# Down products of sequences 1 to 3 as three fp32r passes, with their place in the order moved

## Chip, core and metric

The kernel runs on one core of a Trainium2 chip. The metric is the device time of one execution in microseconds. The engines are TensorE (PE, with its weight loads PEld), VectorE (DVE), ScalarE (ACT), GpSimd (POOL) and SyncE (SP); each has its own queue of instructions and runs it in order, and semaphores tie them together.

## What is computed

Input is x of shape 4 x 1024 x 128: four sequences of 1024 tokens with 128 features. Four layers are added to it, each on a layer norm of x:

```python
x = x + attn_a(_layernorm(x))   # conv, pooled attention, small MLP; per sequence
x = x + ffn(_layernorm(x))      # 8 experts, summed: silu(x @ wg) * (x @ wu) @ wd, 128 -> 512 -> 128
x = x + attn_b(_layernorm(x))   # 16 heads, ALiBi
x = x + ffn(_layernorm(x))      # the same weights again
```

The end of attn_a is what the change touches:

```python
h = _ln(x, ln_boom_g, ln_boom_b)
h = gelu(h @ Wb.T + bb)         # 128 -> 512
x = x + (h @ Wu.T + bu)         # 512 -> 128: the down product
```

All is float32. The kernel runs many products as three fp32r passes: each operand is split into a high part (a cast to fp32r) and a low part (the rest), and hi·hi, hi·lo and lo·hi are summed in PSUM. Others are one plain fp32 matmul.

## The kernel before

Tokens go in 8 tiles of 512. The first ffn walks the tiles in four pairs (function `pair`, kinds first, middle, middle, last). A tile has 32 chunks of 128 hidden features (8 experts x 4), so a pair has 64 steps, 0 to 63. In step p each engine's program has a fixed piece. PE runs the gate and up products of chunk p + 2 (L1132 to L1134, six fp32r matmuls) and then the down product of chunk p (L1139 to L1141, three); it starts the latter when h_hi and h_lo of chunk p are there. ACT runs the silu of chunk p + 1 (L1609) and the cast h_hi of chunk p (L1627). DVE runs the product `hid` of chunk p + 1 (L2059) and the low part h_lo of chunk p (L2080).

Beside pair i the kernel computes attn_a of sequence i + 1, piece by piece (`sequence_step`). Sequence 0 runs ahead of the ffn, its second half partly in the first steps of pair 0 (table `LEFT`). A half u is 512 tokens. At which step a piece stands is written by hand in the table `AT` (first half, second half), to which the first pair adds `SHIFT_FIRST` = 10 and the middle pairs add 3. On every engine the piece stands behind the ffn work of the step, except on PE, where it stands ahead of it.

The pieces that matter here: `up`, four products per half into PSUM, each 128x512 (first half one per step, second half all four in one step); their bias is added by ACT or DVE on the way into `gel`, which lies in the memory `work`; `gelu`, one ACT instruction over 128x2048 of `gel` (L1533), with a table load ahead of it and another ahead of the next silu; `down` (L974), four fp32 matmuls of 128x512 summed in one bank: first half at 42, all four in one step, second half two in each of steps 44 and 45; then `y` (DVE adds bias and residual), `T13` (PE transposes), `x1` (DVE adds into x). `gelu` stands at 36 and 41. In the middle pairs that is: second Gelu in step 44, first half's down in 45, second half's in 47 and 48. In the first pair each is 7 later: 51, 52, 54, 55. `NORM_AT` says at which step the layer norm of the next tile starts (its statistics on DVE); it needs x1 of that tile, and its result is needed by PE in step 62.

The normalised input of the `up` products lies as high part in `h2T` and low part in `h2_lo`; both are free once the last `up` product has run. POOL has little to do in this stretch: two steps of each inner norm, three kinds of 128x512 operations per half (L699, L702, L706), and the reciprocal root of each tile norm. In the last pair it computes 20 of the h_lo (L807).

## Time and profile before

| | us |
|---|---|
| median of 3 runs | 1729.06 |
| lowest, highest | 1727.78, 1729.42 |
| the profiled execution's own time | 1728.12 |
| its span, first to last instruction | 1726.0 |
| PE busy | 1643.9 (95%) |
| DVE busy | 1247.0 (72%) |
| ACT busy | 1042.8 (60%) |
| POOL busy | 254.2 (15%) |

The three pairs with a sequence beside them reach from about 66 to 577 us of the span.

How to read the rows further down. A row of the timeline is: start in us, duration in us, engine, line, operation, what it writes <- what it reads, shapes, xN if N instructions are merged, and in brackets the idle time of the engine ahead of it and who ended it. Durations of matmuls are modelled and overlap, so a pace is read from the distance between starts. A row of the table by stretch is: stretch, its length, then for PE, PEld, DVE, ACT and POOL the busy time and the number of instructions, then the clock that TensorE was granted (1.00 is its 2.4 GHz level, 0.50 its 1.2 GHz level), the DMA share and GB/s. A row by line is: line, engine, operation, names, shapes, count | busy us, mean ns of one | idle time before it and who ended it.

### The profile page before, as it was taken

To read this page: it belongs to the slowest core of one execution; us is meant where nothing else is said; L and a number is where in the kernel's file an instruction comes from. 1 tells how busy PE (TensorE), PEld (TensorE's weight loads), DVE (VectorE), ACT (ScalarE), POOL (GpSimd) and SP (SyncE) were. 2 spreads that over 40 slices of the span, in tenths; PEclk is the share of its full clock that TensorE was granted. 3 is DMA by queue.
4 is the path that set the end of the run, shared out by engine and by line. 5 is a ranking of instruction groups with operands and counts; after the bars stand their busy time and mean duration, and the time that the engine had idled before them with its cause. 6 is when DMAs were issued, how large, how long until landed. Compare 5 with 4: busy or idle time off the path is not lost.

```text
span 1726.0 us, 28181 instructions
## 1 busy us (share of the span) xinstructions
PE 1643.9 (95%) x10321; PEld 1128.6 (65%) x10321; DVE 1247.0 (72%) x2150; ACT 1042.8 (60%) x1692; POOL 254.2 (15%) x471
## 2 busy tenths in 40 slices
PE   5899999999999999989999999989999999999998
PEld 3567777777777876643333333336888888888886
DVE  6678577766866777778888888874666666666665
ACT  6445755565565555567777777776555555555554
POOL 6522001200210013422212112111000000000000
PEclk8999999999999999989999999999999999999999
DMA  7000001002000023223112111100000000000000
GB/s 220 1 0 1 1 20 42 0 1 51 15 1 1 23 88 109 87 79 94 41 48 62 28 51 54 36 4 1 1 7 7 1 7 7 1 7 1 7 7 6
DMA packets 63427, 52.44 MB, mean 30 GB/s; under 512 B 7984, under 2 KB 58559, under 8 KB 63295
## 3 DMA queue, kind: packets, MB, share of 16 engines
q1 hardware_dynamic: 63120, 50.57, 10.1%
q8 instruction: 87, 1.43, 0.3%
q14 instruction: 46, 0.37, 0.1%
q10 hardware_dynamic: 174, 0.07, 0.0%
HBM read 32.40 MB, written 18.22 MB: 29 GB/s over the span
## 4 chain that ended last, share of the span: by engine, by line
PE 80%; DVE 12%; ACT 4%; issue 2%; POOL 1%; DVEq 0%; ACTq 0%; POOLq 0%
PE ps L1283 7%; PE ps L1281 7%; PE ps L1282 7%; PE ps L1244 6%; PE ps L1132 6%; PE ps L1134 6%; PE ps L1133 5%; DVE negm L2049 4%; PE ps L1109 4%; PE ps L1084 4%; PE ps L851 4%; PE ps L1307 3%; PE ps L1305 3%; PE ps L1306 3%; PE ps L1139 3%; PE ps L1141 3%
## 5 line engine op out<-in xcount | busy, mean ns | idle before, releaser
L2190 DVE SCALAR_TENSOR_TENSOR hid<-sg,ps 128x512 f32<-128x512 f32 x256 | 176.0, 687 | 186.3 <-PE ps L1283 185.2
L1694 ACT ACTIVATE sg<-ps 128x512 f32<-128x512 f32 x256 | 153.4, 599 | 239.3 <-PE ps L1283 237.6
L2059 DVE TENSOR_TENSOR hid<-sg,ps 128x512 f32<-128x512 f32 x256 | 174.9, 683 | 167.8 <-PE ps L1134 123.6
L1609 ACT ACTIVATE sg<-ps 128x512 f32<-128x512 f32 x256 | 153.5, 600 | 226.5 <-PE ps L1134 223.7
L2049 DVE TENSOR_REDUCE negp<-ps 128x2 f32<-128x1024 f32 (+2 forms) x224 | 249.4, 1147 | 43.3 <-PE ps L1072 21.5
L1603 ACT ACTIVATE pr<-ps 128x1024 f32<-128x1024 f32 (+2 forms) x208 | 197.1, 958 | 73.2 <-PE ps L1072 37.5
L1132 PE MATMUL ps<-xn_hi,w_hi 128*128 128x512 f32 x512 | 214.5, 419 | 2.0 <-DVE xn_lo L1825 2.0
L1281 PE MATMUL ps<-xn_hi,w_hi 128*128 128x512 f32 x512 | 203.2, 397 | 0.0
L1134 PE MATMUL ps<-xn_hi,w_lo 128*128 128x512 f32 x512 | 201.9, 394 | 0.0
L1283 PE MATMUL ps<-xn_hi,w_lo 128*128 128x512 f32 x512 | 201.7, 394 | 0.0
L1133 PE MATMUL ps<-xn_lo,w_hi 128*128 128x512 f32 x512 | 201.6, 394 | 0.0
L1282 PE MATMUL ps<-xn_lo,w_hi 128*128 128x512 f32 x512 | 200.7, 392 | 0.0
L2080 DVE TENSOR_TENSOR h_lo<-hid,h_hi 128x512 fp32r<-128x512 f32 x236 | 177.3, 751 | 0.0
L2195 DVE TENSOR_TENSOR h_lo<-hid,h_hi 128x512 fp32r<-128x512 f32 x256 | 175.2, 684 | 0.1
L1627 ACT CAST h_hi<-hid 128x512 fp32r<-128x512 f32 x256 | 157.2, 614 | 0.4 <-DVE hid L2059 0.4
L1700 ACT CAST h_hi<-hid 128x512 fp32r<-128x512 f32 x256 | 156.9, 613 | 0.4 <-DVE hid L2190 0.4
L1109 PE MATMUL ps<-qs,ks 63*128 63x512 bf16 (+2 forms) x720 | 113.2, 331 | 20.6 <-DVE negm L2049 12.5
L1109 PEld LDWEIGHTS ps<-qs,ks 63*128 63x128 bf16 x720 | 37.2, 93 | 144.6 <-issue 79.2
L1084 PE MATMUL ps<-ks,qs 60*128 60x512 bf16 (+2 forms) x720 | 114.4, 330 | 10.3 <-ACT pr L1603 6.5
L1603 ACT ACTIVATE pr_third<-ps 128x1024 f32<-128x1024 f32 (+2 forms) x112 | 100.9, 901 | 28.3 <-PE ps L1072 22.2
L1132 PEld LDWEIGHTS ps<-xn_hi,w_hi 128*128 128x128 f32 x512 | 96.6, 189 | 29.9 <-issue 9.8
L736 POOL TENSOR_TENSOR lnw<-mv,eps 128x4 f32<-128x4 f32 x16 | 4.1, 257 | 747.2 <-DVE mv L1806 747.2
(252 smaller groups left out, 3029.6 us busy)
## 6 DMA issues: line engine op xcount, KB each, us to landing
qs<-qd SPq DMA_DIRECT2D x60, 96.0 KB
ks<-kd SPq DMA_DIRECT2D x60, 96.0 KB
kd<-qkp SPq DMA_DIRECT2D x14, 256.0 KB, 2.9
qd<-qkp SPq DMA_DIRECT2D x7, 384.0 KB, 2.5
w_raw<-in_Wg SPq DMA_DIRECT2D x4, 512.0 KB, 7.5
w_raw<-in_Wu SPq DMA_DIRECT2D x4, 512.0 KB, 7.6
w_raw<-in_Wd SPq DMA_DIRECT2D x4, 512.0 KB, 8.6
work<-hd SPq DMA_DIRECT2D x8, 256.0 KB, 5.0
```

The lines of the kernel that those rows point to most:

```text
L1084: mm = pe.matmul(dst[e], q_of(n)[r, hp, i * P:(i + 1) * P], k_of(n)[r, hp, kc * NT:kc * NT + w], start=True, stop=not diag)
L1109: mm = pe.matmul(dst[e], k_of(n)[r, hp, j * P:(j + 1) * P], q_of(n)[r, hp, from_q:from_q + w], start=True, stop=st not in MASKED)
L1132: pe.matmul(dst, w_hi[m][:, w], xn_hi[:, h, :], start=True, stop=False)
L1133: pe.matmul(dst, w_hi[m][:, w], xn_lo[:, h, :], start=False, stop=False)
L1134: pe.matmul(dst, w_lo[m][:, w], xn_hi[:, h, :], start=False, stop=True).then_inc(f[sig], 1)
L1281: pe.matmul(dst, w_hi[m][:, w], xn_hi[:, h, :], start=True, stop=False)
L1282: pe.matmul(dst, w_hi[m][:, w], xn_lo[:, h, :], start=False, stop=False)
L1283: pe.matmul(dst, w_lo[m][:, w], xn_hi[:, h, :], start=False, stop=True).then_inc(f[sig], 1)
L1603: a.activation(pr_of(n, st)[:].rearrange("p (e a) q -> p e a q", e=2)[:, :, hps[0]:hps[-1] + 1, 0:WIDTH[st]], heads(buf, hps, WIDTH[st]), ...
L2049: v.tensor_reduce(to[:, :, hps[0]:hps[-1] + 1, i % SUB], heads(buf, hps, JOB_WIDTH[k]), AX.X, ALU.max, negate=True).then_inc(T["reduced"], 1)
L2080: v.tensor_tensor(h_lo[:, c % 2, :], hid[:, c % 4, :], h_hi[:, c % 2, :].bitcast(F32), ALU.subtract).then_inc(f["hlo"], 1)
L2190: v.scalar_tensor_tensor(hid[:, q % 4, :], sg[:, q % 2, :], 2.0, bank(up_bank(q)), ALU.mult, ALU.mult).then_inc(f["prod"], 1)
```

## The change

The down products of sequences 1 to 3 run as three fp32r passes each (new L1010 to L1012 in place of L974). For that the 512x128 weights are split once in the first pair (`w_down_hi` by ACT in step 20, `w_down_lo` by DVE in step 22, both in memory where the transposed weights lay). The Gelu's output is split for each of the 8 chunks of 512 tokens of a sequence: ACT casts the high part into the memory of the normalised input (`hidden_hi`: chunks 0 and 1 of a half in `h2T`, 2 and 3 in `h2_lo`), and POOL writes the low part over the Gelu's output (`work_lo`). Table entries: casts and subtractions at 38, 39, 40, 42 and 45, 46, 47, 48; `down` from (42, 44) to (44, 50); `y`, `T13` and `x1` follow it; the second norm of the middle pairs from 16 to 18. `gelu` stays at (36, 41). The counts of some semaphores are shifted to fit.

```diff
       "cumq": (15, 19), "kq": (17, 21), "cumk": (18, 22), "vq": (20, 24),
       "T9": (23, 26), "stats9": (23, 26), "norm9": (29, 30), "T10": (30, 31), "h3": (30, 31),
       "low3": (30, 31),
-      "up": (32, 37), "gelu": (36, 41), "down": (42, 44), "y": (43, 45), "T13": (44, 46),
-      "x1": (44, 46)}
+      "up": (32, 37), "gelu": (36, 41), "down": (44, 50), "y": (45, 51), "T13": (46, 52),
+      "x1": (46, 52)}
 
 
 UP_AT = [AT["up"][0] + c for c in range(4)] + [AT["up"][1]] * 4
 DOWN_AT = [AT["down"][0]] * 4 + [AT["down"][1] + c // 2 for c in range(4)]
 
 SHIFT_FIRST = 10
-NORM_AT = {"first": (12, 24), "middle": (10, 16), "last": (13, None)}
+HIDDEN_AT = ((38, 39, 40, 42), (45, 46, 47, 48))
+NORM_AT = {"first": (12, 24), "middle": (10, 18), "last": (13, None)}
 LOW_LATE = 13
...
     if name == "tok":
         return TOK_AT[u][c]
     if name == "hid1":
...
         return ROOTS_FIRST[name, u]
-    return b * 16 - 6 + 4 * u + (4 if name == "norm5" else 12)
+    return b * 24 - 14 + 4 * u + (4 if name == "norm5" else 12)
+
+
+def hidden_to(b, u, c):
+
+    return b * 24 - 14 + 16 + u * 4 + c + 1
+
+
+def wide_to(b, u, c):
+
+    return 4 + (b - 1) * 8 + u * 4 + c + 1
...
 SEQ_BIAS_AT, SEQ_PAR_AT, SEQ_HI_AT, SEQ_LO_AT = 7, 8, 18, 20
+DOWN_HI_AT, DOWN_LO_AT = 20, 22
 
 
...
-            sb("other_matrices", [P, (T_IN - SEQ_MATS) * P], F32, two)
+            w_down_lo = sb("w_down_lo", [P, 4 * P], F32R, two)
+            w_down_hi = sb("w_down_hi", [P, 4 * P], F32R, two)
             rinv = sb("rinv", [P, S], F32, two)
...
 
-            work = sb("work", [P, 4, S], F32, two)
+            with ExitStack() as one:
+                work = sb("work", [P, 4, S], F32, one)
+            work_lo = sb("work_lo", [P, 4, S], F32R, two)
+            gel_lo = work_lo[:].rearrange("p i (a n) -> p (i a) n", n=NT)
             a0_tok, hc_tok, cq, pq = (work[:, i, :] for i in range(4))
...
 
+        def hidden_hi(c):
+
+            return (h2T if c < 2 else h2_lo)[:, c % 2 * NT:(c % 2 + 1) * NT]
+
...
+                    for c in range(4):
+                        if now("hidden", u, c):
+                            pool.wait_ge(s["seq_wide"], wide_to(b, u, c))
+                            n = u * 4 + c
+                            g.tensor_tensor(gel_lo[:, n, :], gel[:, n, :], hidden_hi(c).bitcast(F32), ALU.subtract
+                                            ).then_inc(s["a_pool"], 1)
...
                             elif c == 0:
-                                pe.wait_ge(s["a_gel"], b * 2 + u)
+                                if first:
+                                    pe.wait_ge(s["a_gel"], 1)
                                 pe.wait_ge(s["a_hid1"], b * 4 + 4)
-                            mm = pe.matmul(bank(4) if ahead else dst, W(T_DOWN + c),
-                                           gel_first[:, c, :] if ahead else gel[:, u * 4 + c, :],
-                                           start=(c == 0), stop=(c == 3))
+                            if first:
+                                mm = pe.matmul(bank(4) if ahead else dst, W(T_DOWN + c),
+                                               gel_first[:, c, :] if ahead else gel[:, u * 4 + c, :],
+                                               start=(c == 0), stop=(c == 3))
+                            else:
+                                w = slice(c * P, (c + 1) * P)
+                                pe.wait_ge(s["a_pool"], hidden_to(b, u, c))
+                                pe.matmul(dst, w_down_hi[:, w], hidden_hi(c), start=(c == 0), stop=False)
+                                pe.matmul(dst, w_down_hi[:, w], gel_lo[:, u * 4 + c, :], start=False, stop=False)
+                                mm = pe.matmul(dst, w_down_lo[:, w], hidden_hi(c), start=False, stop=(c == 3))
                             if c == 3:
...
                                      ACT.Gelu).then_inc(s["a_gel"], 1)
+                    for c in range(4):
+                        if now("hidden", u, c):
+                            act.wait_ge(s["a_gel"], b * 2 + u)
+                            if u == 0:
+                                act.wait_ge(s["a_up"], b * 8 + 8)
+                            else:
+                                act.wait_ge(s["a_dn"], b * 2 + 1)
+                            a.copy(hidden_hi(c), gel[:, u * 4 + c, :]).then_inc(s["seq_wide"], 1)
...
                              scale=col(gain)).then_inc(s["seq_wide"], 1)
+
+            def high_part_of_down():
+
+                act.wait_ge(s["a_conv"], 4)
+                a.copy(w_down_hi[:], wt[:, T_DOWN * P:T_CONV * P]).then_inc(s["seq_wide"], 1)
...
                                 high_part_of_sequences(h * CH + c - SEQ_HI_AT)
+                            if kind == "first" and h * CH + c == DOWN_HI_AT:
+                                high_part_of_down()
...
                                     ).then_inc(s["seq_parts"], 1)
+
+            def low_part_of_down():
+
+                dve.wait_ge(s["seq_wide"], 4)
+                dve.wait_ge(s["a_dn"], 2)
+                v.tensor_tensor(w_down_lo[:], wt[:, T_DOWN * P:T_CONV * P], w_down_hi[:].bitcast(F32), ALU.subtract
+                                ).then_inc(s["seq_parts"], 1)
 
```

**PE around the second Gelu of sequence 2.** Before, from the layer's down product of step 44 to that of step 45; `work` is the Gelu's output, `wt` the weights:

```order
L1139 MATMUL ps<-h_hi,w_hi2 128x512
L1140 MATMUL ps<-h_lo,w_hi2 128x512
L1141 MATMUL ps<-h_hi,w_lo2 128x512
L974 MATMUL ps<-work,wt 128x512 x4
L1132 MATMUL ps<-xn_hi,w_hi0 128x512
L1133 MATMUL ps<-xn_lo,w_hi0 128x512
L1134 MATMUL ps<-xn_hi,w_lo0 128x512
L1132 MATMUL ps<-xn_hi,w_hi1 128x512
L1133 MATMUL ps<-xn_lo,w_hi1 128x512
L1134 MATMUL ps<-xn_hi,w_lo1 128x512
L1139 MATMUL ps<-h_hi,w_hi2 128x512
```

The same stretch with the change:

```order
L1175 MATMUL ps<-h_hi,w_hi2 128x512
L1176 MATMUL ps<-h_lo,w_hi2 128x512
L1177 MATMUL ps<-h_hi,w_lo2 128x512
L1168 MATMUL ps<-xn_hi,w_hi0 128x512
L1169 MATMUL ps<-xn_lo,w_hi0 128x512
L1170 MATMUL ps<-xn_hi,w_lo0 128x512
L1168 MATMUL ps<-xn_hi,w_hi1 128x512
L1169 MATMUL ps<-xn_lo,w_hi1 128x512
L1170 MATMUL ps<-xn_hi,w_lo1 128x512
L1175 MATMUL ps<-h_hi,w_hi2 128x512
L1176 MATMUL ps<-h_lo,w_hi2 128x512
L1177 MATMUL ps<-h_hi,w_lo2 128x512
```

The four products between the two down products of the layer are gone from here; they stand two steps further on, as twelve fp32r matmuls. In the changed kernel the layer's lines are L1168 to L1170 and L1175 to L1177.

**ACT around the second Gelu of sequence 2.** Before, steps 43 to 45:

```order
L1609 ACTIVATE sg<-ps 128x512
L1627 CAST h_hi<-hid 128x512
L1609 ACTIVATE sg<-ps 128x512
L1627 CAST h_hi<-hid 128x512
L1533 ACT_TABLE_LOAD
L1533 ACTIVATE work<-work 128x2048
L1609 ACT_TABLE_LOAD
L1609 ACTIVATE sg<-ps 128x512
L1627 CAST h_hi<-hid 128x512
```

With the change (ACT's ffn lines are L1658 and L1676, the Gelu L1569, the new casts L1578):

```order
L1658 ACTIVATE sg<-ps 128x512
L1676 CAST h_hi<-hid 128x512
L1578 CAST h2_lo<-work 128x512
L1658 ACTIVATE sg<-ps 128x512
L1676 CAST h_hi<-hid 128x512
L1569 ACT_TABLE_LOAD
L1569 ACTIVATE work<-work 128x2048
L1658 ACT_TABLE_LOAD
L1658 ACTIVATE sg<-ps 128x512
L1676 CAST h_hi<-hid 128x512
L1578 CAST h2_lo<-work 128x512
```

The third cast of the half stands ahead of the second Gelu's step, the fourth behind the silu and h_hi that follow it; the Gelu itself has kept its place.

**ACT behind the first Gelu of sequence 2.** Before, from the table load back to the h_hi of step 41:

```order
L1609 ACT_TABLE_LOAD
L1609 ACTIVATE sg<-ps 128x512
L1627 CAST h_hi<-hid 128x512
L1609 ACTIVATE sg<-ps 128x512
L1627 CAST h_hi<-hid 128x512
```

With the change:

```order
L1658 ACT_TABLE_LOAD
L1658 ACTIVATE sg<-ps 128x512
L1676 CAST h_hi<-hid 128x512
L1658 ACTIVATE sg<-ps 128x512
L1676 CAST h_hi<-hid 128x512
L1578 CAST h2T<-work 128x512
```

The first cast stands behind the h_hi of step 41; POOL's first subtraction waits for it.

## Rows read from the trace of the kernel before

**Rows 1.** The page, busy time of each engine over the span

```profile
PE 1643.9 (95%) x10321; PEld 1128.6 (65%) x10321; DVE 1247.0 (72%) x2150; ACT 1042.8 (60%) x1692; POOL 254.2 (15%) x471
```

**Rows 2.** Busy time by stretch, around the down products of sequence 2

```profile
340.00:410.00 70.00, 69.66 (x294) 53.39 (x293) 43.27 (x77) 41.44 (x66) 1.21 (x2) 1.00 0.00 1
```

**Rows 3.** Timeline, steps 44 to 46 of pair 1: second Gelu, first half's down

```profile
360.77 1.28 ACT L1533 ACT_TABLE_LOAD   x1
...
362.07 1.91 ACT L1533 ACTIVATE work<-work 128x2048 f32<-128x2048 f32 x1
362.22 0.39 PE L1139 MATMUL ps<-h_hi,w_hi 128*128 128x512 f32 x1
...
362.92 3.59 PE L974 MATMUL ps<-work,wt 128*128 128x512 f32 x8
...
364.00 1.28 ACT L1609 ACT_TABLE_LOAD   x1
...
365.29 0.60 ACT L1609 ACTIVATE sg<-ps 128x512 f32<-128x512 f32 x1
...
365.79 0.61 ACT L1627 CAST h_hi<-hid 128x512 fp32r<-128x512 f32 x1
...
366.60 0.69 DVE L2080 TENSOR_TENSOR h_lo<-hid,h_hi 128x512 fp32r<-128x512 f32 x1
...
367.74 0.61 ACT L1627 CAST h_hi<-hid 128x512 fp32r<-128x512 f32 x1
367.74 0.39 PE L1139 MATMUL ps<-h_hi,w_hi 128*128 128x512 f32 x1
...
368.55 0.68 DVE L2080 TENSOR_TENSOR h_lo<-hid,h_hi 128x512 fp32r<-128x512 f32 x1
...
369.82 0.39 PE L1139 MATMUL ps<-h_hi,w_hi 128*128 128x512 f32 x1
```

**Rows 4.** Timeline, steps 6 and 7 of pair 0: second Gelu of sequence 0

```profile
83.98 0.39 PE L1139 MATMUL ps<-h_hi,w_hi 128*128 128x512 f32 x1
...
84.68 1.62 PE L868 MATMUL ps<-par,wt 128*128 128x1 f32 x14
...
88.35 0.68 DVE L2080 TENSOR_TENSOR h_lo<-hid,h_hi 128x512 fp32r<-128x512 f32 x1
...
89.18 0.47 PE L1139 MATMUL ps<-h_hi,w_hi 128*128 128x512 f32 x1 [1.39 <-ACT h_hi L1627]
```

**Rows 5.** Timeline, steps 40 and 41 of pair 1, behind the first Gelu

```profile
353.47 0.61 ACT L1627 CAST h_hi<-hid 128x512 fp32r<-128x512 f32 x1
...
355.07 0.69 DVE L2080 TENSOR_TENSOR h_lo<-hid,h_hi 128x512 fp32r<-128x512 f32 x1
...
355.90 0.47 PE L1139 MATMUL ps<-h_hi,w_hi 128*128 128x512 f32 x1 [0.19 <-DVE h_lo L2080]
```

**Rows 6.** Timeline, pair 0: a POOL operation and a VectorE low part

```profile
155.21 1.28 POOL L699 TENSOR_TENSOR work<-work,rinv 128x512 f32<-128x512 f32 x1 [1.82 <-DVE work L1897]
...
155.63 1.41 DVE L2080 TENSOR_TENSOR h_lo<-hid,h_hi 128x512 fp32r<-128x512 f32 x1
```

**Rows 7.** Groups by line: POOL's low parts in the last pair

```profile
L807 POOL TENSOR_TENSOR h_lo<-hid,h_hi 128x512 fp32r<-128x512 f32 x20 | 25.7, 1283 | 26.3 <-ACT h_hi L1627 26.3
```

**Rows 8.** Timeline of PE at the end of the first ffn

```profile
750.63 0.66 PE L851 MATMUL ps<-ident,yS 128*128 128x128 f32 x4 [1.83 <-ACT yS L1658]
...
755.11 0.27 PE L1092 MATMUL ps<-identb,mq 128*48 128x128 bf16 x1 [2.94 <-POOL mq L774]
```

**Rows 9.** Busy time and granted clock by stretch, at three gaps

```profile
88.00:90.00 2.00, 0.82 (x4) 0.71 (x5) 2.00 (x4) 1.16 (x3) 0.00 (x0) 1.00 0.00 0
752.00:756.00 4.00, 1.06 (x11) 0.51 (x11) 2.41 (x12) 2.26 (x4) 3.62 (x9) 0.71 0.43 153
756.00:760.00 4.00, 3.15 (x24) 1.43 (x24) 3.94 (x7) 1.94 (x2) 0.33 (x1) 0.50 0.93 309
764.00:768.00 4.00, 3.92 (x30) 0.94 (x29) 2.34 (x4) 2.35 (x4) 0.00 (x0) 1.00 0.56 150
```

## What I expect of it

> **What bounds the kernel now.** I began with the page. TensorE (PE) is busy 1643.9 us of a span of 1726.0 us; no other engine comes near (DVE 72%, ACT 60%) [rows 1]. An average over stages doesn't settle the stretch that the change touches, so I asked for the busy time of the stretch in which the down products of sequence 2 lie. There PE is busy 69.66 of 70 us, ScalarE (ACT) 41 us, VectorE (DVE) 43 us and GpSimd (POOL) 1.2 us, at a granted clock of 1.00 [rows 2]. So every microsecond of PE work or of PE waiting added there moves the end, and every one taken away is a gain.
>
> The next view is the timeline around the down products. The first matmul of the layer's own down product (L1139) marks each step. An undisturbed step is 369.82 − 367.74 = 2.08 us for nine fp32r matmuls [rows 3], 0.231 us each. (The durations in the rows, 0.39 us, overlap; only distances between starts count.) The step that holds the four fp32 products of the first half is 367.74 − 362.22 = 5.52 us [rows 3].
>
> The reader should see one more thing there. Between 360.77 and 365.29 us ACT does nothing for the layer: table load 1.28, Gelu of the second half 1.91, table load back 1.28 us. Only then come the silu, the high part h_hi, DVE's product and its low part h_lo, which ends at 366.60 + 0.69 = 367.29 us [rows 3]. PE can't run its own down product of this step before that. It starts it at 367.74 us without having waited: the four fp32 products were exactly the work that lay over ACT's absence.
>
> **The change, part by part.**
>
> Price of a product. Four fp32 products cost 5.52 − 2.08 = 3.44 us, 0.86 each. Three fp32r passes of the same shape cost 3 × 0.231 = 0.693 us. Saved: 0.167 us a product, 24 products: 4.0 us. The Trainium skill (page "FP8 and Floating Point Precision") counts true FP32 as four passes through the array. That alone would make a product 4 × 0.231 = 0.92 us and the saving 5.5 us; the trace has 0.86, and I use the trace.
>
> The move of the first half. Its products go two steps later, while the second Gelu stays where it was. Between the layer's down product of the step before and that of the next, in the Gelu's shadow, PE now has only six gate and up matmuls, 6 × 0.231 = 1.39 us. The trace of before has this case: at sequence 0's second Gelu no down product lies beside it. There the distance between the two L1139 is 89.18 − 83.98 = 5.20 us, although PE filled part of it with 14 tiny bias matmuls; h_lo was late and PE sat idle 1.39 us [rows 4]. The length is ACT's and DVE's chain, not PE's: the same chain in [rows 3] ends at 367.29 us, and 0.15 us later (as from 88.35 + 0.68 to 89.18 in [rows 4]) PE could start, 367.44 − 362.22 = 5.2 us. So the step shrinks only from 5.52 to 5.20 us, with PE idle about 5.20 − 2.08 = 3.1 us in it (some 2.9 in the record, as the matmul ends overlap), and the four products are paid again in full two steps later, 4 × 0.693 = 2.77 us. First half, per sequence: −0.32 + 2.77 = +2.45 us.
>
> The move of the second half. Six steps later there is no Gelu and nothing waits for it soon: it only gets cheaper, 4 × 0.167 = −0.67 us. T13 and x1 follow by one step as before; the norm of the next tile is moved two steps and its input is needed some ten steps on.
>
> Together +1.78 us a sequence, +5.3 us for three.
>
> The 24 casts on ACT. One costs 0.61 us, and ACT starts every 0.50 us when it has work (365.29 to 365.79) [rows 3]. A step of 2.08 us has two ACT instructions of this kind; a third fits. The fourth cast of the first half comes behind silu and h_hi of the stalled step, so it delays only the next silu, by 0.5 us, for which PE's own late restart leaves room. Price: 0. Without that cover it would be up to 0.5 us a cast.
>
> The 24 subtractions on POOL. POOL's 128x512 subtraction takes 1.28 us [rows 7]. Here DVE pays. DVE's h_lo (two inputs in SBUF) takes 0.69 us alone [rows 3], but 1.41 us when it starts inside a POOL operation of this kind: POOL ran from 155.21 to 156.49, and h_lo, begun at 155.63, ended at 157.04 us, 0.55 us after POOL [rows 6]. So the price depends on when POOL starts. In an undisturbed step h_hi starts with L1139 (both 367.74), so the new cast would end 0.50 + 0.61 = 1.11 us after it; h_lo has then been running since 0.81 us (368.55) [rows 3]. POOL comes behind it, at about 1.5 us, and is done at 2.8, before the next h_lo at 2.08 + 0.81 = 2.9: no cost. At the step of the first cast it is different, since DVE is late there. ACT has h_hi at 353.47, the cast would run until about 354.6, POOL from 354.65 to 355.9. DVE's h_lo starts at 355.07, and PE already waits for it (0.19 us of idle at 355.90) [rows 5]. Blocked, it ends at 355.92 + 0.55 = 356.47 instead of 355.75 us: +0.7 us on PE, of which the next step's small wait gives back 0.1. I take +0.6 us a sequence, 1.9 us in all. Bounds: 0 (if POOL comes behind h_lo everywhere) and 0.7 + 7 × 0.3 = 2.8 us a sequence, 8.4 in all (every other h_lo blocked too; an undisturbed h_lo ends at 368.55 + 0.68 = 369.23 us, 0.6 before L1139 and so 0.4 before PE would notice, which leaves 0.3 of the 0.7).
>
> One-off work in the first pair: a cast and a subtraction of 128x512 for the weights, 0.6 and 0.7 us, in steps in which PE has no wait: 0. DVE's subtraction isn't near a long POOL operation.
>
> **Sum.** 5.3 + 1.9 = +7.2 us. The profiled execution took 1728.12 us, so by the sum 1735.3. The median of the runs shown is 0.94 us above it; on that scale 1729.06 + 7.2 = 1736.3 us.
>
> **Rivals.**
>
> *No lock cost.* If the subtractions always come behind h_lo, only the move is paid: 1729.06 + 5.3 = 1734.4 us. For: the undisturbed steps leave a gap just large enough. Against: the late h_lo of [rows 5], which I expect to be caught in all three sequences.
>
> *The Gelu stays covered, faster than before.* If PE didn't lose the 3.1 us, only the saving would be left: −4.0 us, 1725.1 us. It decides at a loss of 8 × 0.167 = 1.3 us a sequence: below that the change wins. It would need DVE's h_lo of the step to end 1.8 us earlier than in [rows 4], though the same ACT instructions stand ahead of it. I see nothing that does it.
>
> *The clock falls.* The three new gaps of some 2.9 us are the longest in the sequences' stretch. At gaps of 1.83 and 2.94 us around 752 us [rows 8] the granted clock fell: 0.71 on average over 752 to 756 us, 0.50 behind it, 1.00 again from 764, so about 10 us at half; at the single gap of 1.39 us it stayed at 1.00 [rows 9]. Where PE is the bound, 10 us at the 1.2 GHz level do 5 us of work, so one fall costs 5 us: 1736.3 + 5 = 1741.3 us; three: 1751.3 us. For: the length is that of the second gap there. Against: there two gaps came close together, and here full steps of matmuls stand on both sides. The Trainium skill (page "TensorE: Matmul & The Clock Gate", section "Why this matters for your kernels") warns that a long idle gap between bursts takes the clock back to half; by it this rival would be the likeliest.
>
> *ACT falls behind.* If each of the 24 casts reached PE with its 0.5 us: +12 us on top of 5.3, some 1746 us. ACT's 41 of 70 us, plus 8 × 0.5 a sequence, speak against it.
>
> **Chances.** Forecast 0.50; no lock cost 0.22; one or more clock falls 0.13; ACT behind 0.05; Gelu covered 0.05; partly covered, so that gain and loss about cancel, 0.05. A measurement of this kernel can tell about 0.2% (3.5 us) from no change: below 1725.6 is faster, above 1732.5 slower. Faster 0.05, same 0.05, slower 0.90. The range takes in the forecast, the case without lock cost less the scatter of the runs, one clock fall, and the upper bound of the lock cost (1729.06 + 5.3 + 8.4 = 1742.8): 1732.5 to 1743 us.
>
> **What would show it.** Right: in each of the three sequences a gap on PE of about 2.9 us ahead of the layer's own down product, in the step behind the second Gelu's, released by DVE's h_lo or ACT's h_hi; steps of 5.2, 4.85 (2.08 + 2.77) and twice 3.47 us (2.08 + 1.39); h_lo of 1.2 to 1.4 us at the first cast of each sequence with a PE wait of 0.7 to 0.9 us; clock 1.00 throughout. Wrong: no gap behind the Gelu would fell the main term; h_lo always 0.69 us the second; a clock of 0.50 within the sequences' stretch would mean 5 us more each time; PE waiting for ACT's h_hi at several casts would mean that ACT is the bound.

## The result, and the profile with the change

| | before | changed |
|---|---|---|
| median, us | 1729.42 (5 runs) | 1739.05 (5 runs) |
| lowest, highest | 1727.78, 1730.96 | 1737.99, 1741.70 |
| ratio, 95% interval | | 1.0059 [1.0046, 1.0072] |
| profiled execution, its span | 1728.12, 1726.0 | 1741.70, 1739.3 |

The change costs 9.6 us. The page of the changed kernel, busy time of each engine over the span:

```profile
PE 1645.4 (95%) x10345; PEld 1134.0 (65%) x10345; DVE 1253.5 (72%) x2151; ACT 1055.4 (61%) x1717; POOL 288.3 (17%) x495
```

Beside [rows 1], PE is busy only 1.5 us more and the span is 13.3 us longer: most of what was added is waiting. (The 1.5 us is a balance: the three passes save some 4 us of PE's work, and three stretches at the lower clock, below, add some 4.7.) The waiting shows in the busy time by stretch, 70 us around the down products of sequence 2 (columns as in [rows 2]):

```profile
345.00:415.00 70.00, 65.87 (x290) 52.51 (x289) 43.99 (x75) 43.68 (x70) 12.28 (x10) 1.00 0.00 1
```

PE is now idle 4.1 us of the 70, where before it was idle 0.3 us [rows 2]. POOL has 12.3 us to do instead of 1.2. The timeline shows where PE waits. First the step behind the second Gelu of sequence 2 (steps 45 and 46 of pair 1; L1175 is the layer's own down product, L1569 the Gelu, L1676 h_hi, L2138 h_lo, L1578 and L733 the new casts and subtractions; the casts into `h2_lo` appear as h_lo):

```profile
365.97 1.28 ACT L1569 ACT_TABLE_LOAD   x1
...
367.27 1.92 ACT L1569 ACTIVATE work<-work 128x2048 f32<-128x2048 f32 x1
367.42 0.39 PE L1175 MATMUL ps<-h_hi,w_hi 128*128 128x512 f32 x1
...
369.20 1.28 ACT L1658 ACT_TABLE_LOAD   x1
...
370.99 0.61 ACT L1676 CAST h_hi<-hid 128x512 fp32r<-128x512 f32 x1
...
371.80 0.68 DVE L2138 TENSOR_TENSOR h_lo<-hid,h_hi 128x512 fp32r<-128x512 f32 x1
...
372.19 1.44 POOL L733 TENSOR_TENSOR work_lo<-work,h_lo 128x512 fp32r<-128x512 f32 x1 [6.28 <-ACT h_lo L1578]
...
372.63 0.47 PE L1175 MATMUL ps<-h_hi,w_hi 128*128 128x512 f32 x1 [2.96 <-DVE h_lo L2138]
...
374.78 0.40 PE L1175 MATMUL ps<-h_hi,w_hi 128*128 128x512 f32 x1
...
375.47 0.39 PE L1010 MATMUL ps<-h2T,w_down_hi 128*128 128x512 f32 x1
...
379.65 0.40 PE L1175 MATMUL ps<-h_hi,w_hi 128*128 128x512 f32 x1
```

ACT's chain is that of [rows 3]: load, Gelu, load, silu, h_hi, then DVE's h_lo. It ends at 372.48 us. PE had no products to run meanwhile and stood idle for 2.96 us. The step took 372.63 − 367.42 = 5.21 us against 5.52 in [rows 3], the next one 2.15, and the one with the first half's twelve fp32r matmuls 379.65 − 374.78 = 4.87 us.

Then the first cast of the sequence (step 41), which stands against [rows 5]:

```profile
358.35 0.62 ACT L1578 CAST h2T<-work 128x512 fp32r<-128x512 f32 x1
...
359.11 1.29 POOL L733 TENSOR_TENSOR work_lo<-work,h2T 128x512 fp32r<-128x512 f32 x1 [30.21 <-ACT h2T L1578]
...
359.44 1.51 DVE L2138 TENSOR_TENSOR h_lo<-hid,h_hi 128x512 fp32r<-128x512 f32 x1
...
361.10 0.47 PE L1175 MATMUL ps<-h_hi,w_hi 128*128 128x512 f32 x1 [1.02 <-DVE h_lo L2138]
...
361.47 1.49 DVE L2138 TENSOR_TENSOR h_lo<-hid,h_hi 128x512 fp32r<-128x512 f32 x1
```

POOL had started its subtraction at 359.11. DVE's h_lo, begun at 359.44, took 1.51 instead of 0.69 us and ended 0.55 us behind POOL. PE waited 1.02 us for it, before 0.19 [rows 5]. The h_lo after it is caught too (1.49 us), but PE doesn't wait there. The Trainium skill (page "SBUF — State Buffer", section "SBUF: two separate sides") says that VectorE, with two inputs in SBUF, and GpSimd share a port pair as an exclusive lock, held for the whole instruction. The trace agrees: h_lo isn't slowed in proportion, it ends when POOL is done and a little more.

Last, TensorE's granted clock. The falls below are not in the profile of before (busy time and clock by stretch, behind the Gelu's gap of pair 0 and at two places of the attention):

```profile
217.60:221.00 3.40, 3.22 (x8) 2.57 (x9) 1.49 (x3) 0.95 (x3) 1.18 (x1) 0.50 0.00 0
1170.00:1173.20 3.20, 3.20 (x20) 0.26 (x12) 1.01 (x9) 2.19 (x3) 0.00 (x0) 0.50 0.01 4
1187.00:1190.20 3.20, 3.20 (x28) 0.72 (x24) 0.28 (x1) 1.51 (x2) 0.76 (x2) 0.50 0.00 0
```

Three times TensorE ran at its 1.2 GHz level for 3.4 us: from 217.6 us, the very end of the gap of 2.98 us of sequence 1, and from 1169.9 and 1186.9 us in the attention, which the change doesn't touch.

**The account of the profiled execution**, from the distance between the layer's down products step by step (pair 1; pair 2 agrees with it within 0.03 us a step, pair 0 is taken up below):

| step of pair 1 | before | changed | difference |
|---|---|---|---|
| 41: first cast | 2.43 | 3.26 | +0.83 |
| 45: behind the second Gelu | 5.52 | 5.21 | −0.31 |
| 46 | 2.08 | 2.15 | +0.07 |
| 47: first half's products now | 4.24 | 4.87 | +0.63 |
| 48: second half's went from here | 3.78 | 2.08 | −1.70 |
| 52: transposes went from here | 2.51 | 2.08 | −0.43 |
| 53: second half's products, two | 2.08 | 3.47 | +1.39 |
| 54: the other two, and transposes | 2.08 | 3.91 | +1.83 |
| 55: transposes of T13 | 2.08 | 2.51 | +0.43 |
| sum | | | +2.74 |

Three sequences like this: +8.2 us. Pair 0 has the same differences seven steps later and two more: the clock adds 1.55 us at 217.6 us (step 53 took 3.63 instead of 2.08 us), and step 57 is 0.25 us longer, which the run without subtractions, below, has too (0.23) and whose cause isn't shown. So the steps without the clock come to some +8.5 us. The last down product of the first ffn starts 9.9 us later (757.8 against 747.8 us). The other 3.4 us of the span's 13.3 come behind it, with two clock falls of the same length. The profiled execution is the slowest of its five; the median has some 1.1 us on top of 8.5.

### The profile page after: what moved, and what is told of

It is laid out like the page before. It is cut to its first block, busy times and chain, and to the rows that moved or that the text cites. A ratio compares the mean times of both kernels' runs of the same rounds, so it can differ in the third digit from the quotient of the medians.

```text
span 1739.3 us, 28304 instructions
## 1 busy us (share of the span) xinstructions
PE 1645.4 (95%) x10345; PEld 1134.0 (65%) x10345; DVE 1253.5 (72%) x2151; ACT 1055.4 (61%) x1717; POOL 288.3 (17%) x495
## 3 DMA queue, kind: packets, MB, share of 16 engines
q8 instruction: 87, 1.43, 0.3%
## 4 chain that ended last, share of the span: by engine, by line
PE 79%; DVE 12%; ACT 5%; issue 2%; POOL 1%; DMA 0%; DVEq 0%; SPq 0%; ACTq 0%; POOLq 0%
PE ps L1317 7%; PE ps L1318 7%; PE ps L1319 7%; PE ps L1280 6%; PE ps L1168 5%; PE ps L1170 5%; PE ps L1169 5%; PE ps L1145 4%; DVE negm L2107 4%; PE ps L1120 4%; PE ps L879 3%; PE ps L1343 3%; PE ps L1341 3%; PE ps L1342 3%; PE ps L1175 3%; PE ps L1177 3%
## 5 line engine op out<-in xcount | busy, mean ns | idle before, releaser
L1658 ACT ACTIVATE sg<-ps 128x512 f32<-128x512 f32 x256 | 153.5, 600 | 219.7 <-PE ps L1170 216.9
L1168 PE MATMUL ps<-xn_hi,w_hi 128*128 128x512 f32 x512 | 211.6, 413 | 2.0 <-DVE xn_lo L1876 2.0
L1170 PE MATMUL ps<-xn_hi,w_lo 128*128 128x512 f32 x512 | 202.3, 395 | 0.0
L2138 DVE TENSOR_TENSOR h_lo<-hid,h_hi 128x512 fp32r<-128x512 f32 x236 | 183.5, 778 | 0.0
L2255 DVE TENSOR_TENSOR h_lo<-hid,h_hi 128x512 fp32r<-128x512 f32 x256 | 175.0, 683 | 0.1
L1676 ACT CAST h_hi<-hid 128x512 fp32r<-128x512 f32 x256 | 157.2, 614 | 0.4 <-DVE hid L2117 0.4
L1175 PE MATMUL ps<-h_hi,w_hi 128*128 128x512 f32 x256 | 104.4, 408 | 19.4 <-DVE h_lo L2138 14.7
L1168 PEld LDWEIGHTS ps<-xn_hi,w_hi 128*128 128x128 f32 x512 | 96.9, 189 | 28.1 <-issue 8.3
```

The costliest lines, as they stand in the source:

```text
L1168: pe.matmul(dst, w_hi[m][:, w], xn_hi[:, h, :], start=True, stop=False)
L1170: pe.matmul(dst, w_lo[m][:, w], xn_hi[:, h, :], start=False, stop=True).then_inc(f[sig], 1)
L2138: v.tensor_tensor(h_lo[:, c % 2, :], hid[:, c % 4, :], h_hi[:, c % 2, :].bitcast(F32), ALU.subtract).then_inc(f["hlo"], 1)
```

## Experiments

Two theories at the start. **Cover**: the loss comes from the place of the first half's products, which no longer lie over ACT's absence; the lock adds 0.8 us a sequence. **Rival, the splitting**: casts and subtractions (24 each) cost the time, by the lock or on ACT, and the place is secondary. When the clock turned up in the profile a third question was added: what it adds, and whether it hangs on the gap. "Before" in this section is the kernel before, run beside each group on the same chip: median 1729.60 beside the first four (13 runs), 1729.01 beside the next three (21 runs), 1730.47 beside the last two (9 runs).

**The move alone, in fp32.** The kernel before with only the table changed; products stay fp32, there are no casts and no subtractions.

```diff
-      "up": (32, 37), "gelu": (36, 41), "down": (42, 44), "y": (43, 45), "T13": (44, 46),
-      "x1": (44, 46)}
+      "up": (32, 37), "gelu": (36, 41), "down": (44, 50), "y": (45, 51), "T13": (46, 52),
+      "x1": (46, 52)}
...
-NORM_AT = {"first": (12, 24), "middle": (10, 16), "last": (13, None)}
+NORM_AT = {"first": (12, 24), "middle": (10, 18), "last": (13, None)}
```

> The kernel before with only the table of the change: down at (44, 50), y, T13 and x1 behind it, the middle norm at 18; the products stay plain fp32, with no casts and no subtractions. If the loss is ACT's Gelu that nothing covers any more, the step behind the second Gelu is 5.2 us with a PE gap of 2.9 us in each of the three sequences, the first half's four products cost 3.44 us two steps later, and the kernel is 3 x (5.20 - 5.52 + 3.44) = 9.4 us slower than before, up to 11 us if the clock falls behind one of the gaps. If the loss of the change came from the splitting (casts, subtractions, the lock), this kernel is within 2 us of before.

Measured: 1745.76 us (1744.96 to 1747.28, 4 runs), ratio 1.0096 [1.0081, 1.0111]. The timeline of PE in pair 1:

```profile
373.35 0.77 PE L1139 MATMUL ps<-h_hi,w_hi 128*128 128x512 f32 x1 [2.96 <-ACT h_hi L1627]
...
377.33 0.63 PE L1139 MATMUL ps<-h_hi,w_hi 128*128 128x512 f32 x1
377.75 0.63 PE L1140 MATMUL ps<-h_lo,w_hi 128*128 128x512 f32 x1
...
378.61 4.00 PE L974 MATMUL ps<-work,wt 128*128 128x512 f32 x8
```

The same gap, 2.96 us, without any of the new instructions: it is the place that makes it. The step ahead of it took 5.21 us, 0.31 less than before, while the four fp32 products (3.44 us) are paid again elsewhere: 3.13 us a sequence, 9.4 in all. The rest is clock. Behind the gap the matmuls stand 0.42 us apart (377.33 to 377.75) instead of 0.231, and that in all three sequences:

```profile
219.00:222.40 3.40, 3.40 (x10) 2.62 (x9) 0.91 (x3) 1.10 (x2) 0.00 (x0) 0.50 0.00 0
372.70:379.40 6.70, 6.05 (x13) 4.48 (x14) 2.99 (x5) 1.73 (x4) 0.00 (x0) 0.50 0.00 0
543.30:550.00 6.70, 5.84 (x13) 4.46 (x14) 3.20 (x6) 1.94 (x4) 0.00 (x0) 0.50 0.00 0
```

3.4, 6.8 and 6.8 us at half, 17 us in all. A microsecond at half does 0.231/0.43 = 0.54 us of work, so 17 us cost some 7.8. Over the stretch of the first ffn this kernel lost 16.9 us (counted from the first down product to the last), which leaves 16.9 − 9.4 = 7.5 for the clock. The move was as expected; the clock was far under-sized. So the place alone is worse than the whole change, by 16 us against 10. Only about 1 us of that difference is in the steps (9.4 against 8.5: the three passes save 4.0 us and the lock takes 2.5 back). The rest, some 5 us, goes with the longer time at the lower clock: each of this kernel's four runs has a mean granted clock of 0.986, against 0.989 to 0.991 in the five of the changed kernel. Why the clock falls longer here isn't shown. The rival is out all the same: the loss is there without any of the splitting.

**The Gelu follows its products.** The changed kernel with the second Gelu two steps later as well, so that it stands again one step ahead of the first half's products.

```diff
-      "up": (32, 37), "gelu": (36, 41), "down": (44, 50), "y": (45, 51), "T13": (46, 52),
+      "up": (32, 37), "gelu": (36, 43), "down": (44, 50), "y": (45, 51), "T13": (46, 52),
```

> The changed kernel with one number changed: the second Gelu goes two steps later with the products, 43 in place of 41. By the theory of the uncovered Gelu the gap of 2.9 us shrinks to about 0.3 us (a chain of 5.20 us against 2.08 + 2.77 us of work), which takes off 2.8 us a sequence, 8.4 us in all, and the fall of the clock (1.6 us) with it: about the time of before, within 2 us. If the gap is caused by the new casts or subtractions around it, it stays, and so does the time of the changed kernel, 9 to 10 us above before.

Measured: 1730.31 us (1728.11 to 1732.56, 10 runs), ratio 1.0005 [0.9995, 1.0014]: the loss is gone, and so is the gain. PE in pair 1:

```profile
367.71 0.40 PE L1175 MATMUL ps<-h_hi,w_hi 128*128 128x512 f32 x1
...
368.40 0.39 PE L1010 MATMUL ps<-h2T,w_down_hi 128*128 128x512 f32 x1
...
370.96 0.39 PE L1012 MATMUL ps<-h_lo,w_down_lo 128*128 128x512 f32 x1
...
372.92 0.47 PE L1175 MATMUL ps<-h_hi,w_hi 128*128 128x512 f32 x1 [0.18 <-DVE h_lo L2138]
```

From 367.71 to 372.92 us it is the same 5.21 us, but now with the twelve fp32r matmuls in it and a gap of 0.18 us. The granted clock was 1.00 throughout the stretch. It also shows why three passes bring so little here. A step with a Gelu in it is 5.2 us long as long as PE has less than that to do: of the 4 × 0.167 = 0.67 us that the first half's products save, only 0.31 arrives. The first cast still costs 0.83 (step 41: 3.26 us). Per sequence: −0.31 for the first half, −0.64 for the second, +0.83 for the stall and +0.08 in the step behind the Gelu's (2.16 for 2.08), in all −0.04 us. Saving and stall cancel.

**No subtractions.** The changed kernel with POOL's subtractions cut to 4 columns; the second pass multiplies the high part again. The low part of the Gelu's output is left out.

```diff
-                            g.tensor_tensor(gel_lo[:, n, :], gel[:, n, :], hidden_hi(c).bitcast(F32), ALU.subtract
+                            g.tensor_tensor(gel_lo[:, n, 0:4], gel[:, n, 0:4], hidden_hi(c)[:, 0:4].bitcast(F32), ALU.subtract
...
-                                pe.matmul(dst, w_down_hi[:, w], gel_lo[:, u * 4 + c, :], start=False, stop=False)
+                                pe.matmul(dst, w_down_hi[:, w], hidden_hi(c), start=False, stop=False)
```

> The changed kernel with POOL's 24 subtractions cut to 4 columns each; PE's second pass multiplies the high part again, so the low part of the Gelu's output is left out of the result. All waits, casts and matmuls stay. If POOL's subtraction blocks DVE's h_lo, the step of the first cast falls from 3.26 to 2.43 us, the PE gap there from 1.0 to 0.2 us, and the kernel gains 0.8 to 0.9 us a sequence on the changed one, 2.4 to 2.7 us: 7 us above before in place of 9.6. If the cost at that step is ACT's cast, nothing changes there.

Measured: 1741.04 us (1739.18 to 1742.86, 4 runs), ratio 1.0068 [1.0053, 1.0083]. The timeline at the first cast of sequence 1 (step 48 of pair 0):

```profile
205.22 0.20 POOL L733 TENSOR_TENSOR work_lo<-work,h2T 128x4 fp32r<-128x4 f32 x1 [29.40 <-ACT h2T L1578]
...
205.55 0.68 DVE L2138 TENSOR_TENSOR h_lo<-hid,h_hi 128x512 fp32r<-128x512 f32 x1
...
206.38 0.47 PE L1175 MATMUL ps<-h_hi,w_hi 128*128 128x512 f32 x1 [0.20 <-DVE h_lo L2138]
```

With POOL at 0.20 us, h_lo takes 0.68 us and PE waits 0.20, as in [rows 5]; the step is back from 3.25 to 2.44 us. So POOL's long subtraction is the cause of this stall, with its size, and not ACT's cast, which is still there. That it acts through a lock isn't shown by this run; the times above fit it. But the median didn't fall with it. The profile shows the clock at 0.50 behind all three gaps (3.4, 3.4 and 6.8 us) and once in the attention. The local reading held and the total missed: the time at the lower clock was longer here (17.1 us in the sequences' stretch and the attention against 10.2 in the changed kernel's profile), which costs more than the 2.5 us in question. The table at the end of this section takes the clock out.

**The gap filled.** The changed kernel with 12 idle fp32r matmuls where the products stood before. They write a free bank and are used by nobody.

```diff
+    if name == "cover":
+        return AT["gelu"][1] + 1
...
+                    if u == 1 and not first and now("cover", 1):
+                        pe.wait_ge(s["a_hid1"], b * 4 + 4)
+                        for k in range(12):
+                            pe.matmul(bank(6), w_down_hi[:, 0:P], xn_hi[:, 1, :], start=(k == 0), stop=(k == 11))
```

> The changed kernel with 12 idle fp32r matmuls of 128x512 (2.77 us, into a free PSUM bank, read by nobody) on PE in the step behind the second Gelu, where the first half's products used to be. If that step's length is the chain through ACT and DVE, it stays at 5.2 us although PE now has 4.85 us of work in it, and the PE gap shrinks to 0.3 us. The granted clock then stays at 1.00 from 64 to 760 us in the profile, so the kernel is no slower than the changed one and up to 1.6 us faster (the cost of one fall). If the clock's fall at 217 us has nothing to do with the gap, it is seen here too. If the step were bound by PE after all, the kernel would be 8.3 us slower than the changed one.

Measured: 1739.10 us (1736.49 to 1740.15, 4 runs), ratio 1.0054 [1.0040, 1.0069]. PE in pair 1, and the clock behind the filled gaps of sequences 1 and 2:

```profile
365.51 0.40 PE L1181 MATMUL ps<-h_hi,w_hi 128*128 128x512 f32 x1
...
366.20 2.94 PE L1000 MATMUL ps<-xn_hi,w_down_hi 128*128 128x512 f32 x12
...
370.72 0.47 PE L1181 MATMUL ps<-h_hi,w_hi 128*128 128x512 f32 x1 [0.21 <-DVE h_lo L2144]
```

```profile
216.00:222.00 6.00, 5.79 (x26) 4.47 (x25) 4.04 (x6) 3.04 (x6) 1.44 (x1) 1.00 0.00 0
370.00:377.00 7.00, 6.79 (x30) 5.23 (x29) 3.32 (x5) 2.32 (x5) 1.44 (x1) 1.00 0.00 0
```

12 more matmuls cost nothing: the step is 370.72 − 365.51 = 5.21 us as in the changed kernel, so its length is ACT's and DVE's chain, and PE's time in it is free. The clock stayed at 1.00 at all three places. The account of the first ffn is then +8.55 us, the 8.5 of the steps and nothing else. The profile still has two falls in the attention (1166 and 1183 us), and the median is the changed kernel's (1739.10 against 1739.05). The one execution of the four whose mean granted clock was 0.992, as in about half of the executions of before, took 1736.49 us; the others, at 0.990, took 1738.88 to 1740.15.

**The first cast one step later.** The kernel with the Gelu at 43, and the casts and subtractions of the first half at 39 to 42.

```diff
-      "up": (32, 37), "gelu": (36, 41), "down": (44, 50), "y": (45, 51), "T13": (46, 52),
+      "up": (32, 37), "gelu": (36, 43), "down": (44, 50), "y": (45, 51), "T13": (46, 52),
...
-HIDDEN_AT = ((38, 39, 40, 42), (45, 46, 47, 48))
+HIDDEN_AT = ((39, 40, 41, 42), (45, 46, 47, 48))
```

> The kernel with the Gelu moved along (second Gelu at 43), and the casts and subtractions of each first half one step later: 39, 40, 41, 42 in place of 38, 39, 40, 42. By the theory of the lock the first subtraction then no longer meets DVE's late low part: the step of 3.26 us falls to 2.43 us, 0.8 us a sequence, 2.4 us in all, so about 1728 us on the scale where the Gelu alone gave 1730.3 and before 1729.6. If the stall belongs to the cast or subtraction wherever it stands, it moves one step on and nothing is gained.

Measured: 1728.51 us (1726.49 to 1729.88, 11 runs), ratio 0.9996 [0.9987, 1.0005]. Step 41 of pair 1 and the one behind it:

```profile
355.55 0.68 DVE L2138 TENSOR_TENSOR h_lo<-hid,h_hi 128x512 fp32r<-128x512 f32 x1
...
356.38 0.47 PE L1175 MATMUL ps<-h_hi,w_hi 128*128 128x512 f32 x1 [0.20 <-DVE h_lo L2138]
...
356.83 0.68 DVE L2138 TENSOR_TENSOR h_lo<-hid,h_hi 128x512 fp32r<-128x512 f32 x1
...
357.29 1.37 POOL L733 TENSOR_TENSOR work_lo<-work,h2T 128x512 fp32r<-128x512 f32 x1 [32.24 <-ACT h2T L1578]
```

The cast now comes when DVE has caught up. POOL starts behind h_lo's start (357.29 against 356.83), h_lo takes 0.68 us and POOL 1.37. The first-cast stall is gone in all three sequences (step 41 is 2.44 us). From the steps this is −0.83 us a sequence against before (−0.69 in pair 0), −2.4 in all. The median is 0.5 us under before, within the interval of no change. The profiled execution had two clock falls in the attention (1158 and 1175 us), which the profile of before lacks.

**Transposes into the free place.** The same kernel, and the layer's output transposes of the second tile (four 128x128, with DVE's addition two steps behind them) moved from step 35 of the pair into step 46, beside the Gelu.

```diff
+YT_AT = {"first": (3, 21), "middle": (3, 14), "last": (3, 3)}
...
-                            if c == 3:
+                            if c == YT_AT[kind][h]:
...
-                            if c == 5:
+                            if c == YT_AT[kind][h] + 2:
```

> The kernel of the moved Gelu and the later casts, with one more piece of work put over the rest of ACT's absence: the four transposes of the layer's result and DVE's addition behind them go, in the second tile of the first three pairs, from step 35 to the step just ahead of the products (46, in the first pair 53), the addition two steps behind. The gap left there is 5.21 - 4.85 = 0.36 us a sequence, and the transposes cost 0.43 us wherever they stand, so 1.0 us is gained: about 1727 us, 2.5 us under before. If PE's gap was not the bound, nothing is gained.

Measured: 1726.56 us (1724.06 to 1728.53, 11 runs), ratio 0.9983 [0.9975, 0.9992]: 2.5 us under before, a small gain that the interval tells from none. PE in pair 1:

```profile
365.54 0.39 PE L1176 MATMUL ps<-h_hi,w_hi 128*128 128x512 f32 x1
...
366.24 0.60 PE L880 MATMUL ps<-ident,yS 128*128 128x128 f32 x4
366.59 0.48 PE L1011 MATMUL ps<-h2T,w_down_hi 128*128 128x512 f32 x1
...
369.23 0.39 PE L1013 MATMUL ps<-h_lo,w_down_lo 128*128 128x512 f32 x1
...
370.85 0.40 PE L1176 MATMUL ps<-h_hi,w_hi 128*128 128x512 f32 x1
```

There is no gap left in the step, which is now 370.85 − 365.54 = 5.31 us: 0.10 more than before the transposes came in, for 0.42 less in step 36. The step behind it is 0.06 shorter and the next one 0.09 longer, so a sequence is at −1.14 us against −0.83 with the transposes in their old place (pair 0: −0.78 against −0.69). The transposes' share is only 0.7 us in all, of −3.05 us against before. The medians differ by 1.95, and here no clock fall shows in the attention.

**A Gelu of half the width.** The changed kernel, with the second Gelu of sequences 1 to 3 over two of its four chunks. The other two go on without a Gelu. The question was whether a shorter gap keeps the clock.

```diff
-                        a.activation(gel[:, 4 * u:4 * u + 4, :], gel[:, 4 * u:4 * u + 4, :],
+                        n = 2 if u == 1 and not first else 4
+                        a.activation(gel[:, 4 * u:4 * u + n, :], gel[:, 4 * u:4 * u + n, :],
```

> The changed kernel with the second Gelu of sequences 1 to 3 over two of its four chunks (128x1024 in place of 128x2048), so the Gelu of the other two is left out of the result. Everything else stays. The chain through ACT is shorter by half of 1.91 us: the step behind it 4.26 us in place of 5.21, the PE gap 2.0 in place of 2.98 us, 0.95 us a sequence or 2.9 us in all less than the changed kernel (1736 us) without counting the clock. If the length of the gap decides on the clock, it stays at 1.00 behind all three gaps now, which would take off 1 to 3 us more; if any gap of 2 us still brings it down, falls to 0.50 are seen at about 218, 371 or 538 us again.

Measured: 1739.44 us (1738.74 to 1739.97, 4 runs), ratio 1.0057 [1.0042, 1.0072]. The timeline in pair 1, and the clock behind the gaps of sequences 1 and 2 (behind the third, 540 to 546 us, it stayed at 1.00):

```profile
367.58 1.06 ACT L1570 ACTIVATE work<-work 128x1024 f32<-128x1024 f32 x1
367.73 0.39 PE L1175 MATMUL ps<-h_hi,w_hi 128*128 128x512 f32 x1
...
372.09 0.47 PE L1175 MATMUL ps<-h_hi,w_hi 128*128 128x512 f32 x1 [2.11 <-DVE h_lo L2139]
```

```profile
219.00:222.20 3.20, 3.20 (x10) 2.45 (x9) 1.25 (x3) 1.10 (x2) 0.07 (x1) 0.50 0.00 0
372.60:375.80 3.20, 3.20 (x9) 2.45 (x9) 1.04 (x2) 1.10 (x2) 0.48 (x1) 0.50 0.00 0
```

The Gelu took 1.06 us, the step 372.09 − 367.73 = 4.36 us and the gap 2.11: 0.86 us off the Gelu, 0.85 off the step, which shows once more that ACT's chain sets it. That is 2.5 us in three sequences, and the median doesn't show them: against before it stands where the changed kernel stands. The clock fell behind two of the three shorter gaps, and twice in the attention. So a gap of 2.1 us doesn't keep the clock for certain either.

**Both again, side by side.** The changed kernel and the one with the gap filled, unchanged, for more executions of each under the same conditions.

> The changed kernel itself, for more executions and a second profile. If the clock's fall behind the gaps of 2.98 us is a matter of when a gap lies, the second profile shows another number of falls at 218, 372 and 539 us than the first (which had one of three), and the runs' mean clock scatters between 0.986 and 0.992, each 0.001 (3.5 us at half clock) costing up to 1.7 us. A run at 0.992 would take 1736 to 1737 us: 8.2 us over before's runs at 0.992.

> The changed kernel with the 12 idle matmuls in the gap, beside the changed kernel on the same chip. If the gaps bring the clock down in a part of the executions, this kernel has no fall in the profile between 64 and 750 us, and its median lies 1 to 3 us under the changed kernel's. If the falls come from elsewhere (those around 1166 and 1183 us, in the attention), both medians are the same within 1 us.

Measured: changed 1740.36 us (1738.09 to 1741.69, 5 runs), ratio 1.0056 [1.0043, 1.0069]; gap filled 1739.44 us (1738.99 to 1739.92, 5 runs), ratio 1.0052 [1.0039, 1.0066]. The difference of 0.9 us is within the scatter. The changed kernel's clock behind the gaps of sequences 1 and 2 in this execution (behind the third it stayed at 1.00):

```profile
216.20:222.80 6.60, 5.91 (x14) 4.68 (x15) 3.29 (x5) 2.28 (x5) 1.43 (x1) 0.50 0.00 0
373.20:376.40 3.20, 3.20 (x9) 2.43 (x9) 1.31 (x2) 0.91 (x3) 0.76 (x1) 0.50 0.00 0
```

Here it fell behind two of three, for 6.8 and 3.4 us, and not in the attention; but the fall at the end of the first ffn lasted 13.7 us instead of 10.2 (so too in the move in fp32). In the filled kernel it fell behind none, but twice in the attention (1167 and 1184 us).

**The runs at equal clock.** Each execution has its mean granted clock on record, in steps of 0.001. Among the 43 executions of before in this section a step of it goes with about 1.1 us (22 at 0.992 took 1728.5 us on average, 9 at 0.990 took 1730.9). Taking from each execution the average of before's executions with the same clock gives what is left without the clock; beside it stands what the steps of the profile give over the first ffn, with 0.46 us taken off for each microsecond at half:

| kernel | executions | against before at equal clock, us | from the steps, us |
|---|---|---|---|
| changed | 10 | +9.4 | +8.6, second profile +8.2 |
| gap filled | 9 | +8.5 | +8.5, second profile +8.7 |
| without subtractions | 4 | +7.7 | +5.7 |
| Gelu of half the width | 4 | +7.1 | +6.0 |
| Gelu follows | 10 | +0.2 | −0.1 |
| first cast later | 11 | −2.0 | −2.4 |
| transposes in the free place | 11 | −2.7 | −3.05 |

The order is that of the steps, and the gains that the medians hid (of the later cast, of the missing subtractions, of the shorter Gelu) are there. The four kernels without clock falls in the sequences' stretch agree with their steps within 0.4 us. The three with such falls stand 0.8 to 2 us above theirs; why isn't shown. The values of the clock are coarse and executions of two chips are pooled, so half a microsecond means nothing here.

## Why the prediction was right

The forecast was 1736.3 us and slower, with a range of 1732.5 to 1743; the median is 1739.05. Its mechanism is the one that the traces show. By its steps:

- **Price of a product.** Taken at 0.86 us in fp32, 0.693 in three passes; twelve matmuls take 2.79 us (step 47, 4.87 − 2.08), 0.697 a product. Right. The second half came to −0.64 us a sequence (−0.67 in the sum).
- **The step behind the second Gelu.** 5.52 to 5.2 us, with about 2.9 us of idle PE: measured 5.21 and 2.96. The first half was put at +2.45 us and came to −0.31 + 2.79 = +2.48. That the chain of ACT and DVE alone sets this step is shown in three ways: twelve matmuls more leave it at 5.21 us, the fp32 products without any splitting have the same 5.21, and 0.86 us less Gelu takes 0.85 us off it. The row of sequence 0's Gelu [rows 4] was the right one to price it by.
- **Casts on ACT at 0.** Only the step after the stalled one is 0.07 us longer; a h_lo of 0.85 us is caught by a subtraction there too, and the two aren't separated. Nearly right.
- **The lock.** The right place, in all three sequences, but mis-sized: +0.6 us was taken (of 0.7, less 0.1 given back), it came to +0.83. h_lo took 1.51 us, not 1.41, and nothing was given back in the next step, whose h_lo is caught as well. Bounds of 0 and 2.8 us a sequence held it. Elsewhere the subtraction mostly starts inside h_lo and behind its start, as argued, and it is POOL that waits. Two more h_lo of each sequence are caught all the same, behind the second Gelu (0.85 us) and at the last cast (0.90, in pair 0 1.35 us); PE has no wait of its own at either.
- **Sum of the steps.** +7.2 us expected, +8.5 measured (3 × 2.74, and 0.25 in pair 0): 0.7 of the difference is the lock, 0.2 step 46, 0.2 the products, 0.25 step 57 of pair 0. One of the two steps expected at 3.47 us is 3.91, because transposes of the next tile's norm moved into it; they left step 52, so the sum doesn't change.
- **"Clock 1.00 throughout".** Wrong. The rival of a clock fall was given 0.13. In the profiled executions the granted clock fell behind 9 of 12 gaps of 2.96 to 2.98 us (two profiles of the changed kernel, one each of the move in fp32 and of the kernel without subtractions). The argument against it, that full steps of matmuls stand on both sides, didn't hold. The price of one was too high as well: 10 us at half and 5 us lost were taken from 752 to 764 us [rows 9], while a fall here lasts 3.4 us (sometimes 6.8), and one of 3.4 us costs 1.55. It was luck that these two errors went against each other: three falls at the price of the prediction would have been 1751.3 us, far outside the range, and the changed kernel's two profiles had three and two falls that before's lacks. The rule of the Trainium skill that was weighed there (page "TensorE: Matmul & The Clock Gate", section "Why this matters for your kernels") says that a long idle gap between bursts takes the clock to half; on whether it falls, the trace agrees with the rule and not with me, most of the time.

So the time came out 2.7 us above the forecast: 1.3 from the steps, 0.4 because before's own median was 1729.42 beside it instead of 1729.06, and about 1 us for which the clock is the likely cause, but not the only one: the part ahead of the first down product alone ends at 65.7 to 67.9 us in the eleven profiles. What the clock adds is not settled to better than that. The kernel without gaps in the first ffn isn't measurably faster than the one with them (0.9 us in one pair of runs, 0 against the changed kernel's first five), though at equal clock 0.9 us lies between them too. The two falls in the attention come and go between executions and kernels. They were in the profiles of the changed kernel, its filled versions, the one with the later cast and the one with the short Gelu, and the first of them in the one without subtractions. They weren't in those of before, the move in fp32, the Gelu that follows, the transposes in the gap, nor the changed kernel's second one. What they cost varies: with both, the stretch behind the first ffn was 1.6 to 3.4 us longer than before's, with the one 0.65 us. Same place in the program, same length, no change of code there: what decides it stays open.

What I had said would fell the main term, no gap behind the Gelu, was built as a run (the Gelu that follows), and the loss went with it. The rival "no lock cost" was wrong, since all three sequences have the stall; "ACT falls behind" was wrong too, since no step got longer by more than 0.25 us beside those of the table.

## What to carry to other kernels

When work is moved or made cheaper, ask first what it was covering: here four products, with the six gate and up matmuls of the step, were all that PE could do while ACT was away for two table loads and a Gelu, and a step with such a stall has the length of the stall (5.21 us), whether 0 or 12 more matmuls lie in it. So move the stall with its cover, and put into it what can be had from elsewhere (four transposes of another stage came nearly free there, 0.7 us in all). A long two-input GpSimd operation should start behind VectorE's critical two-input operation, never ahead of it: one step later made a stall of 0.8 us a sequence vanish at no other cost, and that was most of the net gain over before. And where the clock varies from run to run, compare executions of equal clock before a median of a few microseconds is believed.

## What was not expected of the hardware

- The granted clock falls to 0.50 behind single gaps of 2.96 to 2.98 us (9 of 12) and 2.11 us (2 of 3) between full stretches of matmuls; behind the same step with a gap of 0.22 us or less it never fell (0 of 15, in five profiles). A fall lasts 3.4 or 6.8 us here, against 10.2 to 13.7 us at the end of the first ffn [rows 9], and where PE is the bound a microsecond of it costs 0.46.
- POOL's subtraction, 1283 ns in [rows 7], took 1.29 us where it starts first and 1.43 to 1.82 us where it starts inside an h_lo, ending 1.15 us behind it. By line, in the changed kernel, the means over all of them:

```profile
L733 POOL TENSOR_TENSOR work_lo<-work,h_lo 128x512 fp32r<-128x512 f32 x12 | 17.1, 1432 | 27.1 <-ACT h_lo L1578 27.1
L733 POOL TENSOR_TENSOR work_lo<-work,h2T 128x512 fp32r<-128x512 f32 x12 | 16.9, 1412 | 116.7 <-ACT h2T L1578 116.7
```

  It works in both directions: whoever starts first has its usual time, the other is late. The late one ends a little sooner than its whole time behind the first: DVE 0.55 us behind POOL for an operation of 0.68 us, POOL 1.15 us behind DVE (373.63 against 372.48 us) for one of 1.29.
- Two places in the attention, 17 us apart, drop the clock for 3.4 us each in some executions and not in others (at least one of them in 6 of 11 profiles), with no gap of PE over 1.25 us beside them.
